# Up-projection of a routed FFN with the weights as stationary operand, fetched tile by tile

## Chip, core and metric

The kernel runs on one core of one Trainium2 chip. The metric is the device time of one execution in microseconds. Below, TensorE is the matrix engine (PE in the rows, PEld for its weight loads, PEldq and PEq for its sequencer), VectorE is DVE, ScalarE is ACT, GpSimd is POOL and SyncE is SP.

## What is computed

A gated cross-attention block over x (2 x 1024 tokens, 256 wide) and 77 text tokens, and behind it a mixture of 8 experts of which each token takes two. All in fp32. Cut to what matters:

```python
# attention: h = tanh(text[t] + feat[s] + b) for every pair, 77 x 1024 x 256 per batch
rho = einsum('bftd,d->bft', tanh(txt_proj + feat_proj + b), w)
att = softmax(rho + mask); txt_h = att @ text
x = x + tanh(g0) * (tanh(txt_h @ Wcw + bcw) * layernorm(x) + tanh(txt_h @ Wcb + bcb))
# experts on n = layernorm(x); H = 1024, D = 256, E = 8, top 2
probs = softmax(n @ router_w.T); vals, idx = top_k(probs, 2)
for eid in range(8):
    w = sum(where(idx == eid, vals, 0))
    out += w * (gelu(n @ w1[eid].T) @ w2[eid].T)
x = x + tanh(g1) * out
```

## The kernel before

The 2048 tokens are taken in four quarters of 512. A quarter of the attention is 40 blocks k = 0 to 39, each with 128 of the 256 features and four text tokens (one in the last pair of blocks): VectorE adds (sum_block, L783), ScalarE takes the tanh (tanh_block, L479 and L481), TensorE reduces over the features (rho_block, L578). hbuf holds four blocks. While quarter q runs, quarter q-1 is settled between the blocks: softmax, gates, the residual, the second layernorm, the router (L598), the places of the rows. The rows are scattered by POOL into row_scratch, sorted by expert (L432), and a table tells the expert (tab_e) and the first row (tab_r) of each tile of 128 rows. Work between blocks stands in tables written out by hand (PE_F, ACT_F, DVE_F, L281 to L286): at block k of its own engine a step of a tile is issued, and each engine goes through its instructions in order.

There are 41 tiles of 128 rows, i = 1 to 41. Tiles 1 to 4 run in the third quarter, 5 to 8 in the fourth, 9 to 14 each in a step written out, interleaved with the settling of the last quarter, and 15 to 41 in a loop of 13 pairs and a last step. All 8 experts' w1 and w2 lie in SBUF (w1_sb, w2_sb, 8 MB each), loaded once near the start, 16 DMAs of 1 MB (L326, L327).

A tile goes through these operations:

- xs_load (L353, SP): SP waits for meta_ok of the tile two before (a buffer of xs is free), loads the row number into a register and fetches 128 rows of 1060 bytes into xs.
- turn_x (L609, TensorE): two transposes to xsT_ps; turned_x (L930, VectorE) copies them to xsT.
- up (L619): in two halves of 512 hidden columns, each two matmuls with xsT as the stationary operand (128x128) and w1 (128x512) moving. The result in h_ps has the rows on partitions and the hidden units along the bank.
- gelu (L496, ScalarE): twice 512 columns, to hg.
- turn_h (L637): eight transposes of hg to hT_ps; turned_h (L945, VectorE) copies them to hgT in two pieces (L948).
- down (L627): eight matmuls with hgT as the stationary operand and w2 (128x256) moving, summed in y_ps.
- y_out (L934, VectorE): y_ps times the router's weight to y_sb, after the previous add has landed. keep_meta (L941) copies the rows' token numbers and weights, after the add two before has landed.
- add (L436, POOL): an indirect DMA adds y_sb to the rows of out.

In the steady part the engines run this order per step i. TensorE (L670): up(i), turn_x(i+1), down(i-1), turn_h(i). VectorE (L1005): turned_x(i+1), keep_meta(i), turned_h(i), y_out(i-1). In the quarters GELU's halves stand behind blocks (6, 7), (13, 14), (21, 22) and (31, 32), the halves of up behind (4, 5), (11, 12), (19, 20) and (29, 30). hT_ps shares its banks with xsT_ps, so turn_x waits for hT_ok.

Behind the last quarter the settling stands in the steps of tiles 9 to 11: scores, gates and x1 in step 9, x2 and a table in step 10, the router's top2 and place in step 11, then the last table (L1024). SP then writes eight tiles of padding rows (L382) into row_scratch, waits for them and for the scattered rows, and loads xs of tile 15.

Of the kernel before, what the change touches and what calls it, by code (L numbers as in the profile page):

```python
# [97 lines left out]
def flamingo_moe(nc, x, ctxT, mask, columns, scalars, Ws, W, router, w1, w2, out):  # L98
    with ExitStack() as ctx:
# [7 lines left out]
        w1_sb = sb("w1_sb", [P, E, DC, H])  # L107
# [65 lines left out]
        hg = sb("hg", [P, H])  # L173
        hgT = sb("hgT", [P, HC, P])
        y_sb = sb("y_sb", [P, D])

        xp = hg[:].rearrange("p (t d) -> p t d", t=TPQ)
        xnT = hgT[:].rearrange("p c d -> p (c d)").rearrange("p (c k) -> p c k", c=DC)
# [66 lines left out]
        xs_in = [sem("xs_in0"), sem("xs_in1")]  # L245
        xsT_ps_ok = sem("xsT_ps_ok")
# [3 lines left out]
        hT_ps_ok = sem("hT_ps_ok")  # L250
        hT_ok = sem("hT_ok")
# [24 lines left out]
        def steps(**at):  # L276
# [36 lines left out]
        def _(sp):  # L313
# [39 lines left out]
            def xs_load(i, par, half):  # L353
# [3 lines left out]
                sp.dma_start(xs[:, par, :], scratch[bass.ds(r, P), :]).then_inc(xs_in[par], 16)  # L357

# [110 lines left out]
        def _(act):  # L469
# [53 lines left out]
            with act.Fori(0, PAIRS) as n:  # L523
                for u in range(2):
                    gelu(tile_pair(n, u)[0], 0)
                    gelu(tile_pair(n, u)[0], 1)
            gelu(TE - 1, 0)
            gelu(TE - 1, 1)

        @block.tensor  # L530
        def _(pe):
# [534 lines left out]
```

## Time and profile before

| | us |
|---|---|
| median of 3 runs | 667.19 |
| lowest, highest | 666.21, 667.31 |
| span of the profiled execution | 666.7 |

| engine | busy us | share | instructions |
|---|---|---|---|
| TensorE, matmuls | 564.8 | 85% | 2850 |
| TensorE, weight loads | 291.3 | 44% | 2851 |
| VectorE | 405.9 | 61% | 1176 |
| ScalarE | 366.9 | 55% | 365 |
| GpSimd | 114.5 | 17% | 98 |

How to read it: a busy share is a mean over stages with different limits. The ends of matmuls are modelled, so a duration of one matmul is longer than its share of a dense stream; distances between starts tell more. Weight loads overlap matmuls. One fp32 matmul is two records, one fp32 transpose is one. Line numbers are those of the kernel. In the timeline a row is: start us, busy us, engine, line, operation, out<-in, shapes, count, and in brackets the idle time before it and what released it; instructions of one kind in a row are merged, and the matmul's duration of a merged row goes from its first start to its last end.

### The profile page before, as it was taken

To read this page: it belongs to the slowest core of one execution; us is meant where nothing else is said; L and a number is where in the kernel's file an instruction comes from. 1 tells how busy PE (TensorE), PEld (TensorE's weight loads), DVE (VectorE), ACT (ScalarE), POOL (GpSimd) and SP (SyncE) were. 2 spreads that over 40 slices of the span, in tenths; PEclk is the share of its full clock that TensorE was granted. 3 is DMA by queue.
4 is the path that set the end of the run, shared out by engine and by line. 5 is a ranking of instruction groups with operands and counts; after the bars stand their busy time and mean duration, and the time that the engine had idled before them with its cause. 6 is when DMAs were issued, how large, how long until landed. Compare 5 with 4: busy or idle time off the path is not lost.

```text
span 666.7 us, 9922 instructions
## 1 busy us (share of the span) xinstructions
PE 564.8 (85%) x2850; PEld 291.3 (44%) x2851; DVE 405.9 (61%) x1176; ACT 366.9 (55%) x365; POOL 114.5 (17%) x98
## 2 busy tenths in 40 slices
PE   3777685766679988889979988699999999999993
PEld 2312121120123432333333565467777666666773
DVE  4899988988868897788887565122222333222321
ACT  0699999999997997998999312011111111111110
POOL 2000000013001160101250115111111111122111
PEclk9798999698999997899999999799999999999998
DMA  3006993002002012102030133312222221221221
GB/s 117 32 1 250 421 403 72 33 17 97 0 1 49 9 67 56 17 0 47 12 102 23 17 65 95 85 19 38 33 32 32 33 39 32 32 32 32 33 28 19
DMA packets 26426, 42.02 MB, mean 63 GB/s; under 512 B 3840, under 2 KB 23296, under 8 KB 24352
## 3 DMA queue, kind: packets, MB, share of 16 engines
q1 hardware_dynamic: 18768, 31.72, 14.2%
q0 software_dynamic: 7632, 9.98, 9.4%
q8 instruction: 13, 0.21, 0.1%
q14 instruction: 13, 0.11, 0.1%
HBM read 27.31 MB, written 14.38 MB: 63 GB/s over the span
## 4 chain that ended last, share of the span: by engine, by line
PE 45%; issue 14%; DVE 9%; ACT 4%; DMA 4%; POOL 3%; SPq 2%; DVEq 1%; ACTq 0%; POOLq 0%
PE y_bank L632 18%; PE h_ps L622 16%; PE rho L578 5%; PE hT_ps L643 4%; DVE hbuf L783 3%; DMA out<-y_sb,meta 2%; ACT hbuf L479 2%; POOL row_scratch L432 2%; ACT hbuf L481 1%; PE hT_ps L616 1%; DMA xs<-row_scratch 1%; DMA row_scratch<-rows,slot 1%; PE misc L598 1%; POOL out L442 1%; SPq L381 1%
## 5 line engine op out<-in xcount | busy, mean ns | idle before, releaser
L479 ACT ACTIVATE hbuf<-hbuf 128x1536 f32<-128x1536 f32 (+2 forms) x160 | 248.0, 1577 | 31.5 <-DVE hbuf L783 31.2
L783 DVE TENSOR_SCALAR hbuf<-featT,txtb 128x512 f32<-128x512 f32 (+1 forms) x519 | 214.7, 481 | 22.0 <-PE rho L578 21.2
L578 PE MATMUL rho<-hbuf,wpad 128*32 128x512 f32 x1232 | 176.5, 648 | 52.7 <-ACT hbuf L481 29.4
L498 ACT ACTIVATE hg<-h_ps 128x512 f32<-128x512 f32 x82 | 48.8, 596 | 228.6 <-PE h_ps L622 225.4
L632 PE MATMUL y_bank<-w_sb,hgT 128*128 x672 | 158.0, 387 | 2.3 <-DVE y_sb L939 1.6
L622 PE MATMUL h_ps<-w_sb,xsT 128*128 x328 | 151.0, 599 | 0.2
L632 PEld LDWEIGHTS y_bank<-w_sb,hgT 128*128 128x128 f32 x672 | 125.8, 193 | 31.0 <-issue 15.4
L442 POOL DMA_INDIRECT out<-y_sb,meta x42 | 67.7, 1612 | 382.4 <-DVE y_sb L939 309.8
L578 PEld LDWEIGHTS rho<-hbuf,wpad 128*32 128x32 f32 x1232 | 29.3, 112 | 162.9 <-ACT hbuf L481 76.9
L622 PEld LDWEIGHTS h_ps<-w_sb,xsT 128*128 128x128 f32 x328 | 58.6, 191 | 70.2 <-issue 70.2
L948 DVE COPY hgT<-hT_ps 128x512 f32<-128x512 f32 x82 | 52.8, 686 | 46.7 <-PE hT_ps L643 46.0
L481 ACT ACTIVATE hbuf<-featT,txtb 128x512 f32 (+1 forms) x97 | 68.6, 707 | 0.0
L932 DVE COPY xsT<-hT_ps 128x256 f32<-128x256 f32 x41 | 17.4, 424 | 78.8 <-PE hT_ps L616 72.8
L643 PE MATMUL hT_ps<-ident,hg 128*128 128x128 f32 x328 | 43.0, 274 | 1.1 <-DVE xsT L932 1.1
L432 POOL DMA_INDIRECT row_scratch<-rows,slot x32 | 35.2, 1099 | 45.4 <-DVE slot L890 36.9
L943 DVE COPY meta<-xs 128x9 f32<-128x9 f32 x41 | 7.2, 175 | 58.3 <-DMA out<-y_sb,meta 58.3
L643 PEld LDWEIGHTS hT_ps<-ident,hg 128*128 128x128 f32 x328 | 37.7, 141 | 11.3 <-issue 6.7
L939 DVE TENSOR_SCALAR y_sb<-y_bank,meta 128x256 f32<-128x256 f32 x42 | 20.3, 483 | 15.4 <-PE y_bank L632 6.1
L616 PE MATMUL hT_ps<-ident,xs 128*128 128x128 f32 x82 | 17.1, 291 | 13.2 <-DMA xs<-row_scratch 12.9
L616 PEld LDWEIGHTS hT_ps<-ident,xs 128*128 128x128 f32 x82 | 11.0, 147 | 36.6 <-issue 24.4
L567 PE MATMUL misc<-hgT,W_sb 128*128 128x512 f32 x32 | 17.6, 685 | 4.3 <-DVE hgT L770 4.3
L420 POOL TENSOR_TENSOR rstd<-var,negh 128x4 f32<-128x4 f32 x4 | 4.6, 1143 | 67.7 <-DVE var L759 67.7
(125 smaller groups left out, 203.2 us busy)
## 6 DMA issues: line engine op xcount, KB each, us to landing
w_sb<-in_w SPq DMA_DIRECT2D x16, 1024.0 KB, 21.9
xs<-row_scratch SPq DMA_DIRECT2D x41, 132.5 KB
row_scratch<-pad SPq DMA_DIRECT2D x17, 132.5 KB, 18.4
hg<-in_x SPq DMA_DIRECT2D x4, 512.0 KB, 3.5
x_res<-in_x SPq DMA_DIRECT2D x4, 512.0 KB, 4.7
out<-x_res SPq DMA_DIRECT2D x4, 512.0 KB
out<-y_sb,meta POOLq DMA_INDIRECT x42
row_scratch<-rows,slot POOLq DMA_INDIRECT x32
```

The costliest lines, as they stand in the source:

```text
L432: g.indirect_dma_start(out=scratch, out_offset=bass.IndirectOffsetOnAxis(ap=slot[:, k, t:t + 1], axis=0), in_=rows[:, t, :], in_offset=Non ...
L442: g.indirect_dma_start(out=out, out_offset=bass.IndirectOffsetOnAxis(ap=meta[:, par, 0:1].bitcast(I32), axis=0), in_=y_sb[:], in_offset=No ...
L479: ins = s.activation(h, h, ACT.Tanh)
L481: ins = s.activation(hbuf[:, k % HB, j, :], featT[:, c, bass.ds(q, 1), :].rearrange("p o t -> p (o t)"), ACT.Tanh, bias=txtb[:, c, bb, CG ...
L498: s.activation(hg[:, 512 * c:512 * (c + 1)], h_ps[:, 512 * c:512 * (c + 1)], ACT.Gelu).then_inc(hg_ok, 1)
L578: ins = t.matmul(rho[32 * j:32 * j + 32, :], wpad[:, c, 31 - r:63 - r], hbuf[:, k % HB, j, :], start=(k == 0), stop=(last and c == DC - 1) ...
L616: ins = t.transpose(xsT_ps[:, c * P:(c + 1) * P], xs[:, par, c * P:(c + 1) * P], ident[:])
L622: ins = t.matmul(h_ps[:, 512 * c2:512 * (c2 + 1)], xsT[:, c, :], w1_sb[:, bass.ds(e, 1), c, 512 * c2:512 * (c2 + 1)], start=(c == 0), stop ...
L632: ins = t.matmul(y_ps, hgT[:, c, :], w2_sb[:, bass.ds(e, 1), c, :], start=(c == 0), stop=(c == HC - 1))
L643: ins = t.transpose(hT_ps[:, c * P:(c + 1) * P], hg[:, c * P:(c + 1) * P], ident[:])
L783: ins = v.tensor_scalar(hbuf[:, k % HB, j:j + 1, :], featT[:, c, bass.ds(q, 1), :], txtb[:, c, bb, CG * r + j:CG * r + j + 1], None, ALU.add)
L948: v.tensor_copy(hgT[:].rearrange("p c k -> p (c k)")[:, 512 * c2:512 * (c2 + 1)], hT_ps[:, 512 * c2:512 * (c2 + 1)]).then_inc(hT_ok, 1)
```

## The change

The activated tile is produced with the hidden units on partitions, the form in which down needs it. up has w1 as the stationary operand and the turned rows xsT as the moving one: per tile 16 matmuls of 128x128 with 128 columns moving, eight chunks k of 128 hidden units. So turn_h, turned_h, hg, hT_ps and their semaphores are gone; hgT gets two buffers. gelu is one instruction over 1024 columns, placed where its first half stood, and waits for y_ok as well, since it now writes hgT. w1 no longer lies in SBUF as a whole: w1_st holds two tiles' worth, and SP fetches the 1 MB of a tile's expert behind the tile's rows, after gelu of the tile two before. up waits for that fetch and no longer loads the expert into a register. xsT_ps has a bank of its own, and turn_x waits for xsT_ok.

```diff
-        w1_sb = sb("w1_sb", [P, E, DC, H])
+        w1_st = sb("w1_st", [P, 2, DC, H])
-        hg = sb("hg", [P, H])
-        hgT = sb("hgT", [P, HC, P])
+        hgT = sb("hgT", [P, 2, HC, P])
-        hT_ps = bank("hT_ps", 2)
+        xsT_bank = bank("xsT_bank")
-        PE_F = steps(up0=(4, 11, 19, 29), up1=(5, 12, 20, 30), down0=(7, 14, 22, 32), down1=(8, 15, 23, 33),
-                     turn_h=(9, 17, 25, 35))
+        PE_F = steps(up0=(4, 11, 19, 29), up1=(5, 12, 20, 30), down0=(7, 14, 22, 32), down1=(8, 15, 23, 33))
-        ACT_F = steps(gelu0=(6, 13, 21, 31), gelu1=(7, 14, 22, 32))
-        DVE_F = steps(x=(10, 17, 30, 35), meta=(9, 16, 27, 36), y=(12, 19, 28, 37), h=(14, 21, 29, 39))
+        ACT_F = steps(gelu=(6, 13, 21, 31))
+        DVE_F = steps(x=(10, 17, 30, 35), meta=(9, 16, 27, 36), y=(12, 19, 28, 37))
@@ SP
-                sp.dma_start(w1_sb[:, e], w1[:, e]).then_inc(w_in, 16)
...
                 sp.dma_start(xs[:, par, :], scratch[bass.ds(r, P), :]).then_inc(xs_in[par], 16)
+                e = sp.value_load(tab_e[0:1, bass.ds(i, 1)], min_val=0, max_val=E - 1)
+                if not (isinstance(i, int) and i <= 2):
+                    sp.wait_ge(hg_ok, i - 1)
+                sp.dma_start(w1_st[:, par], w1[:, bass.ds(e, 1)].rearrange("p o c m -> p (o c) m")).then_inc(w1_in[par], 16)
@@ ScalarE
-            def gelu(i, c):
-                act.wait_ge(h_ps_ok, 2 * (i - 1) + c + 1)
-                s.activation(hg[:, 512 * c:512 * (c + 1)], h_ps[:, 512 * c:512 * (c + 1)],
-                             ACT.Gelu).then_inc(hg_ok, 1)
+            def gelu(i, par):
+                act.wait_ge(h_ps_ok, i)
+                act.wait_ge(y_ok, i)
+                s.activation(hgT[:, par].rearrange("p c k -> p (c k)"), h_ps[:], ACT.Gelu).then_inc(hg_ok, 1)
@@ TensorE
-            def up(i, c2, e):
-                pe.wait_ge(xsT_ok, i)
-                for c in range(DC):
-                    ins = t.matmul(h_ps[:, 512 * c2:512 * (c2 + 1)], xsT[:, c, :],
-                                   w1_sb[:, bass.ds(e, 1), c, 512 * c2:512 * (c2 + 1)],
-                                   start=(c == 0), stop=(c == DC - 1))
-                ins.then_inc(h_ps_ok, 1)
+            def up(i, par, count, half):
                 if half == 0:
+                    pe.wait_ge(w1_in[par], 16 * count)
+                    pe.wait_ge(xsT_ok, i)
+                    pe.wait_ge(hg_ok, i)
+                for k in range(HC // 2 * half, HC // 2 * (half + 1)):
+                    for c in range(DC):
+                        ins = t.matmul(h_ps[:, k * P:(k + 1) * P],
+                                       w1_st[:, par, c, k * P:(k + 1) * P], xsT[:, c, :],
+                                       start=(c == 0), stop=(c == DC - 1))
+                if half == 1:
+                    ins.then_inc(h_ps_ok, 1)
...
-            def turn_h(i, x_before=True):
-                if x_before:
-                    pe.wait_ge(xsT_ok, i + 1)
-                for c2 in range(2):
-                    pe.wait_ge(hg_ok, 2 * (i - 1) + c2 + 1)
-                    for c in range(HC // 2 * c2, HC // 2 * (c2 + 1)):
-                        ins = t.transpose(hT_ps[:, c * P:(c + 1) * P], hg[:, c * P:(c + 1) * P], ident[:])
-                    ins.then_inc(hT_ps_ok, 1)
@@ VectorE
-            def turned_h(i):
-                for c2 in range(2):
-                    dve.wait_ge(hT_ps_ok, 2 * (i - 1) + c2 + 1)
-                    v.tensor_copy(hgT[:].rearrange("p c k -> p (c k)")[:, 512 * c2:512 * (c2 + 1)],
-                                  hT_ps[:, 512 * c2:512 * (c2 + 1)]).then_inc(hT_ok, 1)
```

down waits for hg_ok instead of hT_ok and reads hgT[:, par].

## Rows read from the trace of the kernel before

**Rows 1.** Stage windows (stretch, length, engines' busy us, clock, DMA), and the page's chain.

```profile
245.00:350.00 105.00, 89.83 (x518) 34.55 (x518) 86.24 (x253) 93.87 (x88) 21.40 (x16) 0.94 0.16 40
435.00:500.00 65.00, 65.00 (x277) 45.38 (x277) 18.97 (x40) 9.57 (x16) 12.40 (x8) 0.99 0.20 31
...
PE y_bank L632 18%; PE h_ps L622 16%; PE rho L578 5%; PE hT_ps L643 4%; DVE hbuf L783 3%; DMA out<-y_sb,meta 2%; ACT hbuf L479 2%; POOL row_scratch L432 2%; ACT hbuf L481 1%; PE hT_ps L616 1%; DMA xs<-row_scratch 1%; DMA row_scratch<-rows,slot 1%; PE misc L598 1%; POOL out L442 1%; SPq L381 1%
```

**Rows 2.** Timeline of one steady step, 559 to 569 us.

```profile
559.32 1.55 POOL L442 DMA_INDIRECT out<-y_sb,meta  x1 [6.44 <-DVE y_sb L939]
...
560.59 3.62 PE L632 MATMUL y_bank<-w_sb,hgT 128*128 x16
...
563.00 0.17 DVE L943 COPY meta<-xs 128x9 f32<-128x9 f32 x1 [1.78 <-DMA out<-y_sb,meta]
...
564.05 1.04 PE L643 MATMUL hT_ps<-ident,hg 128*128 128x128 f32 x8
...
564.92 3.60 PE L622 MATMUL h_ps<-w_sb,xsT 128*128 x8
...
566.04 0.48 DVE L939 TENSOR_SCALAR y_sb<-y_bank,meta 128x256 f32<-128x256 f32 x1
...
567.29 1.55 POOL L442 DMA_INDIRECT out<-y_sb,meta  x1 [6.43 <-DVE y_sb L939]
...
568.36 0.38 PE L616 MATMUL hT_ps<-ident,xs 128*128 128x128 f32 x2
```

**Rows 3.** Window from down's start to down's start, L948's copies alone on VectorE.

```profile
440.84:640.43 199.59, 32.24 (x50) 1.00 0.21 34
```

**Rows 4.** Timeline of router and gate projection, and both by line (busy us, mean ns).

```profile
393.76 1.86 PEld L598 LDWEIGHTS misc<-rT,x2T 128*128 128x128 f32 x16 [1.82 <-DVE x2T L850]
...
20.68 1.25 PE L548 MATMUL h_ps<-x2T,x_res 128*128 128x160 f32 x8
...
L598 PEld LDWEIGHTS misc<-rT,x2T 128*128 128x128 f32 x64 | 7.4, 191 | 5.4 <-DVE x2T L850 5.4
...
L548 PE MATMUL h_ps<-x2T,x_res 128*128 128x160 f32 x8 | 1.2, 299 | 0.0
```

**Rows 5.** Timeline of the third quarter: up1 and GELU of tiles 3 and 4.

```profile
233.30 1.98 PE L622 MATMUL h_ps<-w_sb,xsT 128*128 x4
...
234.32 0.60 ACT L498 ACTIVATE hg<-h_ps 128x512 f32<-128x512 f32 x1
...
259.74 0.60 ACT L498 ACTIVATE hg<-h_ps 128x512 f32<-128x512 f32 x1 [1.99 <-PE h_ps L622]
...
260.63 1.98 PE L622 MATMUL h_ps<-w_sb,xsT 128*128 x4
...
262.65 0.60 ACT L498 ACTIVATE hg<-h_ps 128x512 f32<-128x512 f32 x1 [0.51 <-PE h_ps L622]
```

**Rows 6.** Timeline of the third quarter: ScalarE behind two hgT copies.

```profile
216.59 1.49 ACT L479 ACTIVATE hbuf<-hbuf 128x1536 f32<-128x1536 f32 x1 [1.42 <-DVE hbuf L783]
```

**Rows 7.** Timeline of the stretch behind the last quarter, 380 to 437 us.

```profile
380.30 0.48 DVE L939 TENSOR_SCALAR y_sb<-y_bank,meta 128x256 f32<-128x256 f32 x1
...
381.53 1.56 POOL L442 DMA_INDIRECT out<-y_sb,meta  x1 [14.51 <-DVE y_sb L939]
...
386.72 0.17 DVE L943 COPY meta<-xs 128x9 f32<-128x9 f32 x1 [0.87 <-DMA out<-y_sb,meta]
...
429.07 0.69 PE L616 MATMUL hT_ps<-ident,xs 128*128 128x128 f32 x2 [6.16 <-DMA xs<-row_scratch]
...
429.92 6.56 PE L632 MATMUL y_bank<-w_sb,hgT 128*128 x16 [0.16 <-issue]
```

**Rows 8.** Timeline of the end: y_out of tile 40.

```profile
653.58 0.48 DVE L939 TENSOR_SCALAR y_sb<-y_bank,meta 128x256 f32<-128x256 f32 x1
```

**Rows 9.** DMA issues (KB each, us to landing) and the page's GB/s by slice.

```profile
hg<-in_x SPq DMA_DIRECT2D x4, 512.0 KB, 3.5
...
GB/s 117 32 1 250 421 403 72 33 17 97 0 1 49 9 67 56 17 0 47 12 102 23 17 65 95 85 19 38 33 32 32 33 39 32 32 32 32 33 28 19
```

More of the change, by code:

```diff
@@ L506, in quarter @@
                     if tiles and k in ACT_F:
-                        m, step = ACT_F[k]
-                        gelu(tile(q, m)[0], int(step[-1]))
+                        gelu(*tile(q, ACT_F[k][0])[:2])
             quarter(0, 0, False, False)
@@ L524, in _ @@
                 for u in range(2):
[L525 to L528, printed above, removed]
+                    gelu(*tile_pair(n, u)[:2])
+            gelu(*tile_at(TE - 1)[:2])
         @block.tensor
@@ L607, in settle, with turn_x @@
                              stop=True).then_inc(count_ps_ok, 1)
-            def turn_x(i, par, half, late=False):
+            def turn_x(i, par, half):
                 pe.wait_ge(xs_in[par], 16 * half)
-                if late:
-                    pe.wait_ge(hT_ok, 2 * i)
-                elif not (isinstance(i, int) and i == 1):
-                    pe.wait_ge(hT_ok, 2 * (i - 1))
+                if not (isinstance(i, int) and i == 1):
+                    pe.wait_ge(xsT_ok, i - 1)
                 for c in range(DC):
@@ L658, in quarter @@
                     if k in PE_X and (tiles or settling and k == max(PE_X)):
-                        turn_x(*tile(q, PE_X[k] + 1), late=(PE_X[k] == LATE))
+                        turn_x(*tile(q, PE_X[k] + 1))
                     if tiles and k in PE_F:
                         m, step = PE_F[k]
-                        i = tile(q, m)[0]
+                        i, par, count = tile(q, m)
                         if step in ("up0", "up1"):
-                            up(i, int(step[-1]), expert(i))
-                        elif step in ("down0", "down1"):
-                            down(i - 1, int(step[-1]), expert(i - 1))
+                            up(i, par, count, int(step[-1]))
                         else:
-                            turn_h(i, x_before=(m != LATE))
+                            down(i - 1, 1 - par, int(step[-1]), expert(i - 1))
             def step(this, following, mid=lambda: None, late=lambda: None):
-                i = this[0]
-                e = expert(i)
-                up(i, 0, e)
-                up(i, 1, e)
+                i, par, count = this
+                up(i, par, count, 0)
+                up(i, par, count, 1)
                 mid()
@@ L678, in step @@
                 e = expert(i - 1)
-                down(i - 1, 0, e)
-                down(i - 1, 1, e)
+                down(i - 1, 1 - par, 0, e)
+                down(i - 1, 1 - par, 1, e)
                 late()
-                turn_h(i, bool(following))
             pe.wait_ge(setup_sb, DC)
```

34 lines of the change are left out of this document (14 added, 20 removed).

## The prediction

> **What bounds the kernel now.** I read the stage windows first. Up to 370 us the tanh blocks set the pace: from 245 to 350 us ScalarE is busy 93.87 of 105 us, TensorE 89.83, VectorE 86.24, so two other engines stand close behind. From 435 us on TensorE is busy in all of the stage while ScalarE and VectorE are mostly idle, at a granted clock of 0.99 (2.4 GHz) [rows 1]. The chain that ended last says the same: the down-projection (L632) 18% and the up-projection (L622) 16% lead it [rows 1]. So I cost the parts one by one: the 26 steady expert steps behind 437 us, the end, the seam from 370 to 437 us, and the two tiled quarters before it.
>
> **The steady step, before.** The starts of TensorE's groups in one step of the timeline give down(i-1) 560.59 to 564.05 = 3.46 us, turn_h 564.05 to 564.92 = 0.87, up 564.92 to 568.36 = 3.44, and turn_x the rest [rows 2]. The window from one down-projection's start to another holds 50 hgT copies, two a tile, so 25 tiles in 199.59 us: 7.98 us a step [rows 3]. turn_x is 7.98 - 3.46 - 0.87 - 3.44 = 0.21 us. None of the four waits for data.
>
> **The steady step, after.** turn_h goes (-0.87 us), turn_x stays, down keeps its 16 records at 3.46 us (its moving side and weights have the same shapes). An fp32 matmul is two records. up had 4 matmuls, 8 records in 3.44 us, 0.43 us each for 512 columns; it gets 16 matmuls, 32 records of 128 columns. The streaming is the same: 0.43 / 4 = 0.107 us a record, 3.44 us. New is a weight load for every one. The nearest row for a load by itself is the router's, 128x128 fp32 with only 8 columns moving: 16 loads in 1.86 us, one load lasting 0.191, so (1.86 - 0.19) / 15 = 0.111 us apart [rows 4]. The nearest for load beside matmul is the gate projection, 8 records of 160 columns in 1.25 us, one lasting 0.299: (1.25 - 0.30) / 7 = 0.136 us apart, where 160 columns stream in 0.107 x 160 / 128 = 0.134 and a load needs 0.111 [rows 4]. The load is hidden there to 0.002 us. So I take the larger of 0.107 and 0.111: 32 x 0.111 = 3.55 us. Bounds: 0.107 (3.42 us) below; 0.136 above, since 128 columns can hardly take longer than 160 (4.35 us). The step becomes 3.46 + 0.21 + 3.55 = 7.22 us, 0.76 less; between 7.09 and 8.02 by the bounds.
> Twenty-six periods lie between up(15) and up(41): -19.8 us.
>
> What must stay hidden in a step of 7.2 us. GELU in one piece is at most 2 x 0.60 us and can start only when all of up is done; it has the whole down-projection, 3.46 us, before up(i+1) wants h_ps and down(i) wants hgT. Its new wait for y_ok is no later than the one that down(i-1) had already. The two hgT copies (1.29 us a tile) go from VectorE; in this stage they cost only the place of y_out behind them: y_sb starts at 566.04, 2 us after down ended [rows 2]. The loop of the adding store is y_sb 0.48, to POOL's start 0.77, POOL's start to landing 3.7 (559.32 to 563.00): some 5.0 us [rows 2]. It fits in 7.2 with 2.2 to spare, where it had 3.0.
> The w1 fetch is 1 MB a tile on SP's queue. SP waits for meta_ok, loads a register, issues xs, loads another, waits for hg_ok of the tile two before (done by then) and issues w1. Queued behind that wait on SP are the next xs load and, in the quarters, the loads and stores of x; all are wanted later than the gelu waited for. Its length: the weights' loads of 1 MB ran at 421 GB/s in their fullest slice, 2.5 us for 1 MB, and a 512 KB load landed 3.5 us after issue, so about 4.7 us [rows 9]. It is issued about two steps ahead of its use, less the wait for meta: over 6 us are left. I cost it at nothing. If that cover is gone, up waits for w1 and the excess stands on every step.
>
> **The end.** Now: copies, then y_out(40) at 653.58, its add lands, y_out(41), last add [rows 8]. After, y_out(40) starts right behind down(40), which ended some 1.9 us before 653.58 (turn_h and both copies lie between); the rest follows add by add. -1.9 us.
>
> **The seam.** Here VectorE, in order, carries settle steps, hgT copies, y_out and waits for adds. y_out(8) at 380.30 stood behind two copies (-1.6 us) and its add, landed at 386.72, held back x2, the table and y_out(9); further copies stood before y_out(9) and before place [rows 7]. Walking the same chain without copies and turn_h, with up at 3.55, I get y_out(9) 2.7 us, the counts 2.8 us and the end of the table 5 us earlier. Then SP: xs(14), the eight pads, and xs(15), on whose landing turn_x waited until 429.07 [rows 7]. One more register load and issue (w1 of tile 14) stand in front of the pads: +1.1 us, at a register load and an issue of about 0.5 us each, an estimate. So turn_x(15) comes about 4.2 us earlier; down(13) behind it ran at half rate, 6.56 us [rows 7], and will again, since TensorE idles at least as long before. turn_h(14) after it goes, -0.87. Taken: -5 us. Bounds: 0, if w1 traffic slows the adds on that chain by all of it, and -7.
> In that chain the wait for `added` is what ends last, so the slower add (386.72 - 381.5 = 5.2 us after POOL's start, where it is 3.7 in the steady stage) is already in.
>
> **The two tiled quarters.** Gains: 8 hgT copies a quarter go from VectorE, 5.1 us, and 4 x 0.87 us from TensorE, but neither is the leader; what shows is ScalarE's idle time behind them, such as 1.42 us at 216.59 [rows 6]. I count 1.3 us a quarter. GELU in one piece saves one fixed part, about 0.15 us a tile: 0.6.
> Loss: gelu0 stood after block 6 (13, 21, 31), when only up0 was done; the whole GELU now stands there and needs up1, on TensorE behind block 5 (12, 20, 30). In the third tile up1 runs 233.30 to 235.3 and gelu0 ran at 234.32: 1 us of wait. In the fourth, up1 runs 260.63 to 262.6 and gelu0 ran at 259.74, a tanh block between it and gelu1 at 262.65: that block now comes after, about 2.5 us late [rows 5]. The first two tiles I put at 0.3 us each. Sum 4.1, of which the idle time that follows anyway takes about 0.7. Net per quarter 4.1 - 0.7 - 1.9 = +1.5; for two +3 us. Bounds: -3 (all waits absorbed) and +8 (none, no gain).
> The 8 MB less at the start (w1_sb) frees nothing: TensorE asks for the weights only at the third quarter, behind 180 us, while the slices at 421 and 403 GB/s, the fifth and sixth of 40, end at 100 us [rows 9].
>
> **Sum.** Against the profiled execution's 666.7 us: -19.8 - 1.9 - 5 + 3 = -23.7, so 643.0. The span is within 0.5 us of the median of the runs, 667.19; I leave it there.
>
> **Rivals.** A, slower: the load is not hidden at equal length. Where load and stream take 0.111 and 0.107, any record above (7.98 - 3.46 - 0.21) / 32 = 0.135 us makes the step longer than now. With half of the load bare, 0.107 + 0.055 = 0.162: up 5.2 us, step 8.9, +23 us on 26 steps, and some 1.7 us more on the tiles before, partly hidden: about 690. Against it: the 160-column row, 0.136 with everything in it. Chance 5%.
> The Trainium skill, "TensorE: Matmul & The Clock Gate", section "Back-to-back issue gap", has a rule for this rival: the pace of load-and-matmul pairs is set by both, 81 ns at 128 columns where the isolated gap is 56. By its ratio a record would be 0.107 x 81 / 56 = 0.155 us, the step 8.6 and the time about 680, an estimate from that page. Its figures are not for fp32, and the gate projection's row disagrees.
> B, adds become the bound: w1's 2.5 us of transfer falls on the add's own, since w1 is issued about when the previous add has landed. If each add is longer by all of it, the loop is 5.0 + 2.5 = 7.5 us, the step follows it, -0.5 x 26 = -12 and the seam gives only 3: 666.7 - 12 - 1 - 3 + 3 = about 654. For it: the slower 5.2 us add beside other traffic [rows 7]. Against: the two overlap in part only, and an add that comes late delays the next issue of w1 as well. Chance 14%. The Trainium skill, "Trainium Kernel Development and Optimization", section "Key Constraints", says that DMAs from SP's and POOL's queues run on the same 16 engines and interleave, which speaks for B; by full sharing it is the 654 above.
> C, records between 0.120 and 0.136: step 7.5 to 8.0, time 650 to 663. Chance 8%.
> D, the waits in the quarters and the seam cost more (+8, 0): 653. Chance 8%; the other way, 636 and less: 7%.
>
> **How the numbers follow.** The forecast case (638 to 649) has 56%; A 5%, B 14%, C 8%, D 8%, better 7%, and 2% for a w1 fetch that comes late on every step and makes it slower. The range reaches to B and most of D and C: 635 to 657, which leaves out A and the far ends. A measurement of this kernel tells 0.2% (1.3 us) from no change. Faster by more 0.91, within 0.02, slower by more 0.07.
>
> **What would show it.** In a steady step of the changed kernel: 32 records of up in about 3.5 us and starts of down 7.2 us apart; loads 0.11 us apart; no wait of up on w1; gelu within down; y_sb right behind down. y_sb or the down-projection waiting for the add's landing is B. In the quarters, ScalarE idle before GELU released by h_ps, 1 us in the third tile and 2 to 2.5 in the fourth. The wait for xs(15) should end near 425 us plus what the quarters cost. A step over 7.5 us, or a seam that gains nothing, makes the prediction wrong.

## The result, and the profile after

The median went from 667.19 to 656.74 us (5 runs, 655.15 to 665.18); the ratio to the kernel before is 0.985 with the interval 0.982 to 0.988. So the kernel is faster by 10 us where 24 were forecast. The profiled execution of the changed kernel, with a span of 663.4 us, was the slowest of the five, so every comparison of stages below reads `again`, the very same kernel measured a second time (span 653.3 us, median 655.97).

The page of after first: its engines, the traffic by slice, the groups and the transfers with KB each and the time from issue to landing.

```profile
span 663.4 us, 10960 instructions
...
PE 549.6 (83%) x3506; PEld 355.8 (54%) x3507; DVE 356.0 (54%) x1093; ACT 360.4 (54%) x324; POOL 116.4 (18%) x98
...
GB/s 118 32 1 276 344 26 0 33 17 149 75 1 103 20 67 182 80 0 111 8 73 175 79 112 160 211 161 159 159 161 168 173 186 180 162 159 160 166 151 24
...
L498 ACT ACTIVATE hgT<-h_ps 128x1024 f32<-128x1024 f32 x41 | 42.0, 1025 | 238.8 <-PE h_ps L620 228.4
...
L620 PE MATMUL h_ps<-xsT,w_st 128*128 128x128 f32 x1312 | 164.0, 285 | 0.5 <-DMA w_st<-in_w 0.5
...
w_st<-in_w SPq DMA_DIRECT2D x41, 1024.0 KB, 4.9
...
out<-y_sb,meta POOLq DMA_INDIRECT x42, 5.5
```

The transposes, their records and the 82 hgT copies are gone, GELU is one instruction a tile. But in the 27th to 38th slices 159 to 186 GB/s are moved, where it was 19 to 39 [rows 9], and the store that adds to `out` lands 5.5 us after its issue. Up itself waited for w1 only 0.5 us in all. The step is read from the timeline of `again` (columns: start, length, engine, line, operation; in brackets the idle time before it and what ended it):

```profile
562.26 3.76 PEld L620 LDWEIGHTS h_ps<-xsT,w_st 128*128 128x128 f32 x32
562.48 3.73 PE L620 MATMUL h_ps<-xsT,w_st 128*128 128x128 f32 x32
562.70 0.17 DVE L929 COPY meta<-xs 128x9 f32<-128x9 f32 x1 [3.54 <-DMA out<-y_sb,meta]
563.64 0.48 DVE L925 TENSOR_SCALAR y_sb<-y_bank,meta 128x256 f32<-128x256 f32 x1 [0.76 <-DVE meta L929]
563.70 0.34 SPq L352 DMA_DIRECT2D xs<-row_scratch  x1
564.88 1.55 POOL L441 DMA_INDIRECT out<-y_sb,meta  x1 [6.27 <-DVE y_sb L925]
564.88 0.33 SPq L356 DMA_DIRECT2D w_st<-in_w  x1
...
566.05 0.38 PE L609 MATMUL xsT_bank<-ident,xs 128*128 128x128 f32 x2
566.25 1.02 ACT L498 ACTIVATE hgT<-h_ps 128x1024 f32<-128x1024 f32 x1 [6.71 <-PE h_ps L620]
...
566.72 3.71 PE L631 MATMUL y_bank<-w_sb,hgT 128*128 x16 [0.29 <-issue]
...
570.27 2.17 PE L620 MATMUL h_ps<-xsT,w_st 128*128 128x128 f32 x18
570.75 0.17 DVE L929 COPY meta<-xs 128x9 f32<-128x9 f32 x1 [3.85 <-DMA out<-y_sb,meta]
```

Up takes 566.05 - 562.48 = 3.57 us, 0.112 a record, as forecast. Between turn_x and down stand 0.67 us where [rows 2] have 0.21. And the add that POOL starts at 564.88 lands only at 570.75, 5.87 us later, where [rows 2] have 3.7; w1's fetch is issued in the same hundredth of a microsecond as POOL starts. keep_meta waits for that landing on VectorE, and y_sb stands behind it.

By stage, from the starts of the same instructions in each trace (third and fourth quarter from rhoT to rhoT; seam from the last rhoT to turn_x(16); tail from turn_x(16) to turn_x(41); end from there):

| us | start | quarters | seam | tail (a step) | end | span |
|---|---|---|---|---|---|---|
| before | 180.3 | 97.2 + 92.2 | 71.0 | 199.6 (7.98) | 26.5 | 666.7 |
| again | 181.2 | 94.1 + 94.3 | 66.2 | 192.6 (7.70) | 25.0 | 653.3 |
| difference | +0.9 | -1.0 | -4.8 | -7.0 | -1.5 | -13.4 |
| forecast | 0 | +3 | -4.9 | -19.0 | -2.8 | -23.7 |

The forecast row is the prediction's sum, cut at the same places. Its 26 periods run from up(15) to up(41); 25 of them are the tail here, 25 x 0.76 = 19.0, and the 26th lies in two pieces: up(15) (+0.1) in the seam, turn_h(40) (-0.87) in the end. Of the 10.3 us between forecast and trace, the tail misses 12.0, the end 1.3 and the start 0.9; the quarters came out 4.0 better.

### The profile page after: what moved, and what is told of

Its sections match the earlier page's. It is cut to its first block and busy times, and to the rows that moved or that the text cites. A ratio compares the mean times of both kernels' runs of the same rounds, so it can differ in the third digit from the quotient of the medians.

```text
span 663.4 us, 10960 instructions
## 1 busy us (share of the span) xinstructions
PE 549.6 (83%) x3506; PEld 355.8 (54%) x3507; DVE 356.0 (54%) x1093; ACT 360.4 (54%) x324; POOL 116.4 (18%) x98
## 5 line engine op out<-in xcount | busy, mean ns | idle before, releaser
L498 ACT ACTIVATE hgT<-h_ps 128x1024 f32<-128x1024 f32 x41 | 42.0, 1025 | 238.8 <-PE h_ps L620 228.4
L620 PEld LDWEIGHTS h_ps<-xsT,w_st 128*128 128x128 f32 x1312 | 160.1, 200 | 19.8 <-issue 17.4
L631 PE MATMUL y_bank<-w_sb,hgT 128*128 x672 | 163.6, 396 | 7.6 <-issue 5.6
L620 PE MATMUL h_ps<-xsT,w_st 128*128 128x128 f32 x1312 | 164.0, 285 | 0.5 <-DMA w_st<-in_w 0.5
L918 DVE COPY xsT<-xsT_bank 128x256 f32<-128x256 f32 x41 | 17.4, 424 | 74.0 <-PE xsT_bank L609 73.6
L609 PE MATMUL xsT_bank<-ident,xs 128*128 128x128 f32 x82 | 16.4, 282 | 5.7 <-DMA xs<-row_scratch 5.7
L609 PEld LDWEIGHTS xsT_bank<-ident,xs 128*128 128x128 f32 x82 | 10.1, 144 | 11.8 <-DMA xs<-row_scratch 5.9
L419 POOL TENSOR_TENSOR rstd<-var,negh 128x4 f32<-128x4 f32 x4 | 4.6, 1141 | 66.2 <-DVE var L745 66.2
L423 POOL TENSOR_TENSOR rstd<-var,negh 128x4 f32<-128x4 f32 x4 | 5.5, 1378 | 51.4 <-DVE var L824 51.4
L562 PEld LDWEIGHTS misc<-hgT,W_sb 128*128 128x128 f32 x32 | 6.1, 208 | 14.9 <-issue 8.9
L554 PE MATMUL misc<-ident,rows 128*128 128x128 f32 x32 | 7.5, 411 | 4.5 <-DVE rows L750 4.5
## 6 DMA issues: line engine op xcount, KB each, us to landing
row_scratch<-pad SPq DMA_DIRECT2D x17, 132.5 KB, 10.3
```

The source lines that it names most:

```text
L498: s.activation(hgT[:, par].rearrange("p c k -> p (c k)"), h_ps[:], ACT.Gelu).then_inc(hg_ok, 1)
L562: ins = t.matmul(misc[e][:], W_sb[:, c, e * P:(e + 1) * P], xnT[:, c, :], start=(c == 0), stop=(c == DC - 1))
L609: ins = t.transpose(xsT_ps[:, c * P:(c + 1) * P], xs[:, par, c * P:(c + 1) * P], ident[:])
L620: ins = t.matmul(h_ps[:, k * P:(k + 1) * P], w1_st[:, par, c, k * P:(k + 1) * P], xsT[:, c, :], start=(c == 0), stop=(c == DC - 1))
L631: ins = t.matmul(y_ps, hgT[:, par, c, :], w2_sb[:, bass.ds(e, 1), c, :], start=(c == 0), stop=(c == HC - 1))
```

## The experiments

**The same kernel again**, for a second trace. No edit.

> The changed kernel once more, for a profile at an undisturbed clock. Both theories expect 655 to 657 us. The profile so far shows a steady step of 7.71 us, where 7.22 was forecast, and GELU waiting 10.7 us for h_ps in the third quarter. Theory Q (the quarters lose through the place of the GELU) expects rhoT copies 97 to 100 us apart over the third quarter and 95 to 98 over the fourth, 97.2 and 92.2 before. If the quarters' loss was only the lower clock of that execution, they come back to 97 and 92.

Measured 655.97 us, ratio 0.986 (0.982 to 0.989), the table and fence above. The gain comes back, and the step is 7.7 us also here.

**Without w1's traffic.** The fetch stays where it is with its register load, wait and issue, but moves 16 bytes a partition; two experts' w1 are loaded once near the start. The up-projection so takes the wrong experts' w1 for most tiles.

```diff
-  sp.dma_start(w1_st[:, par], w1[:, bass.ds(e, 1)]...)
+  sp.dma_start(w1_st[:, par, 0, 0:4], w1[:, bass.ds(e, 1), 0, 0:4]...)
```

> w1 of experts 0 and 1 is loaded once, and each tile's fetch is cut from 8 KB to 16 bytes a partition, so its issue, its waits and its place on SP stay and its traffic goes (the output is not the reference's: each tile uses the wrong expert's w1). Theory C (a cycle over two steps: the add lands late beside w1, so keep_meta, so the xs load, so TensorE's sequencer gets to turn_x and to the register load for down too late): the add lands 3.7 to 3.9 us after POOL's start instead of 5.4, xs lands 1.5 us earlier, turn_x to down falls from 0.65 to 0.22 us, the step from 7.71 to 7.24, and the time by 26 x 0.47 = 12 us to about 644. Theory S (TensorE's sequencer alone: 32 short load-and-matmul pairs leave it no lead, so the register load for down is bare whatever the DMAs do): the step stays at 7.7 and the time at 655.

Measured 641.04 us (638.8 to 643.9), ratio 0.963 (0.958 to 0.968); step 7.27, turn_x to down 0.22. From its timeline:

```profile
562.03 0.48 DVE L928 TENSOR_SCALAR y_sb<-y_bank,meta 128x256 f32<-128x256 f32 x1 [1.99 <-PE y_bank L634]
562.04 0.34 SPq L358 DMA_DIRECT2D w_st<-in_w  x1
563.28 1.55 POOL L444 DMA_INDIRECT out<-y_sb,meta  x1 [5.70 <-DVE y_sb L928]
...
567.14 0.17 DVE L932 COPY meta<-xs 128x9 f32<-128x9 f32 x1 [1.72 <-DMA out<-y_sb,meta]
```

The add lands 3.86 us after POOL's start, and y_sb waits for down again. So it is the megabyte, not the extra instructions on SP, that costs the 0.43 us a step. It isn't the place of xs either: xs is issued 1.00 us behind keep_meta here as in `again` (means of the steps between 460 and 610 us). How the megabyte costs it, the run doesn't say.

**The fetch alone, in the kernel before.** Everything as before, but w1 fetched a tile at a time behind xs and used as the moving side.

```diff
   sp.dma_start(xs[:, par, :], scratch[bass.ds(r, P), :])...
+  e = sp.value_load(tab_e[...]); sp.wait_ge(hg_ok, 2 * (i - 2) + 1)
+  sp.dma_start(w1_st[:, par], w1[:, bass.ds(e, 1)]...)
...
-  ... w1_sb[:, bass.ds(e, 1), c, 512 * c2:512 * (c2 + 1)]
+  ... w1_st[:, par, c, 512 * c2:512 * (c2 + 1)]
```

> The kernel before with one part of the change alone: w1 fetched tile by tile into two buffers (SP issues it behind xs, after GELU of the tile two before), up in its old form with w1 moving. Theory P: the fetch lengthens the add here too if w1's transfer falls on it, but the step of 7.98 us leaves room (two steps 15.97 against a cycle of about 15.4 or less), so the step stays at 7.98 to 8.05 and the time at 665 to 669. If the fetch has a cost of its own (its issue on SP, the memory's bandwidth, TensorE's reads beside its writes), the step grows by about the 0.45 us that it cost in the changed kernel, and the time to 677.

Measured 667.79 us (666.64 to 668.3), ratio 1.002 (1.000 to 1.004); step 7.98, the add 3.78 us. The same megabyte per tile costs nothing here. What differs is its place:

```profile
563.68 0.34 SPq L362 DMA_DIRECT2D w_st<-in_w  x1
...
565.66 1.55 POOL L447 DMA_INDIRECT out<-y_sb,meta  x1 [6.43 <-DVE y_sb L945]
```

POOL starts 2 us behind w1's issue; in `again` they coincide.

**One part each: a later GELU, and the sequencer's wait.** TensorE's gap before down looked like a cause: its sequencer passes the wait for xs late and the register load for down's expert lies bare behind it. `hoist` loads that register ahead; `late_gelu` moves GELU one block later in the quarters.

```diff
-  ACT_F = steps(gelu=(6, 13, 21, 31))
+  ACT_F = steps(gelu=(7, 14, 22, 32))      # late_gelu
-  if following: turn_x(*following)
   e = expert(i - 1)
+  if following: turn_x(*following)         # hoist
```

> ACT_F places the GELU of a tile one block later, where its second half stood (7, 14, 22, 32). Theory Q: the waits of GELU for h_ps in the quarters (10.7 us in the third) fall to below 2 us, the quarters give back 2 to 3 us each, time 650 to 652. If instead TensorE or VectorE sets the quarters' pace, the wait only moves and the time stays within 1.5 us of 656.

> TensorE's register load for the expert of down stands ahead of turn_x instead of behind it. Cycle theory: TensorE's sequencer gets through the wait for xs only just before turn_x, and the register load behind it is bare, 0.65 us from turn_x to down against 0.22. With the load ahead of the wait, turn_x to down is 0.22 us; the cycle over two steps is 0.43 us shorter, so the step goes from 7.70 to about 7.49, with the rest of the wait now in front of turn_x; time 655.5 - 5 = 650. If the gap is a wait for something else (y_ok, hg_ok), it stays at 0.65 and the time at 656.

late_gelu 655.58 us (0.985, 0.980 to 0.991), hoist 656.44 us (0.985, 0.983 to 0.987): neither moves the time. In hoist the gap is gone, and up waits instead:

```profile
564.13 3.81 PE L620 MATMUL h_ps<-xsT,w_st 128*128 128x128 f32 x32 [0.29 <-DMA w_st<-in_w]
564.59 0.17 DVE L929 COPY meta<-xs 128x9 f32<-128x9 f32 x1 [3.77 <-DMA out<-y_sb,meta]
...
565.53 0.48 DVE L925 TENSOR_SCALAR y_sb<-y_bank,meta 128x256 f32<-128x256 f32 x1 [0.76 <-DVE meta L929]
565.59 0.34 SPq L352 DMA_DIRECT2D xs<-row_scratch  x1
566.77 1.55 POOL L441 DMA_INDIRECT out<-y_sb,meta  x1 [6.27 <-DVE y_sb L925]
566.77 0.33 SPq L356 DMA_DIRECT2D w_st<-in_w  x1
```

The step stays at 7.75: TensorE's waits are symptoms of something that turns with a period of its own.

**w1 issued first.** SP issues w1 (wait hg_ok) ahead of the wait for meta_ok and xs.

```diff
+  e = sp.value_load(...); sp.wait_ge(hg_ok, i - 1); sp.dma_start(w1_st[:, par], ...)
   r = sp.value_load(...); sp.wait_ge(meta_ok, i - 1)
   sp.dma_start(xs[:, par, :], ...)
-  e = sp.value_load(...); sp.wait_ge(hg_ok, i - 1); sp.dma_start(w1_st[:, par], ...)
```

> Only SP's order is turned round: w1 of a tile is issued first (after its wait for GELU), then the tile's xs (after its wait for keep_meta). So far: with the fetch's traffic away the steady step is 7.27 us, with xs loaded early it is 7.25, and in both the add lands 3.8 us after POOL's start (5.55 in the changed kernel, where w1 is issued at the moment of POOL's start). Theory P (phase: what costs is that w1's transfer falls on the add's; issued right behind GELU it is over before the add begins): add to landing 3.8, step 7.25, time 643 to 645, although xs is loaded no earlier relative to its keep_meta. Theory X (what costs is that xs is asked for late, behind keep_meta; early_xs gained by that): xs comes as late as now or later, step 7.6 to 7.8, time 653 to 656.

Measured 658.79 us, ratio 0.988 (0.985 to 0.991): no gain as a whole, where theory P had 643 to 645 us. But the add is 3.80 us, and 21 of the tail's 25 steps are 7.24 to 7.53 us; three of 8.1 to 8.2 bring the mean to 7.43 (7.70 in `again`). The quarters and the seam took back what the tail gave (fourth quarter 98.9, seam 71.1; 94.3 and 66.2 in `again`). In the new order xs has to wait for GELU of two tiles before too, which would explain that; it was not tried apart. From the timeline:

```profile
562.38 1.55 POOL L441 DMA_INDIRECT out<-y_sb,meta  x1 [5.91 <-DVE y_sb L925]
...
565.08 0.33 SPq L352 DMA_DIRECT2D w_st<-in_w  x1
566.27 0.17 DVE L929 COPY meta<-xs 128x9 f32<-128x9 f32 x1 [1.74 <-DMA out<-y_sb,meta]
```

A fetch issued 2.7 us behind POOL's start no longer slows that add, and its own landing is early enough for the next.

**xs freed early.** keep_meta's source is copied behind turned_x, so SP needn't wait for the add.

```diff
-  sp.wait_ge(meta_ok, i - 1)
+  sp.wait_ge(xs_free, i - 2)
   v.tensor_copy(xsT..., xsT_ps).then_inc(xsT_ok, 1)
+  v.tensor_copy(metaq[:, par, :], xs[:, par, D:ROW]).then_inc(xs_free, 1)
-  v.tensor_copy(meta[:, par, :], xs[:, par, D:ROW])
+  v.tensor_copy(meta[:, par, :], metaq[:, par, :])
```

> VectorE copies the rows' tokens and weights out of xs right behind turned_x into a pair of small buffers, so xs is free, and its next load issued, without waiting for an add; keep_meta copies from there. Theory C: the two-step cycle is cut; what is left is the add's own loop, y_sb 0.48 + 0.76 to POOL + 5.4 to landing + 0.17 + 0.79 of register load before the next y_sb = 7.6 us, so the step falls only from 7.71 to about 7.6, unless w1's earlier issue changes the overlap; turn_x to down falls to 0.22. Time about 653. Theory S: turn_x to down stays at 0.65 and the time at 656.

> The kernel of early_xs once more: its four executions came at 642.6, 647.0, 672.1 and 675.1 us, in two groups. If the two groups belong to the kernel, they come back here, some executions near 645 and some near 673; theory P then has a second state of the phase, in which w1 falls on the add in each step. If they belonged to that chip's minute, all come near 645.

Executions were 646.99, 672.12, 642.64, 675.07 us, and the second time 649.5, 646.47, 672.27, 647.2: two groups of the same program, 25 us apart, so no single number stands for it. Both profiles are of the short group: step 7.245, add 3.77 us.

**VectorE's register load.** Behind keep_meta's wait a register load lies bare (0.76 us in `again`). `y_hoist` puts it ahead of y_out's waits, but still behind keep_meta's; `y_hoist_early` joins that with hoist and the early xs, `y_hoist_early_late` with late_gelu besides.

```diff
+  e = dve.value_load(tab_e[...])
   dve.wait_ge(y_ps_ok, i + 1); dve.wait_ge(added, 16 * (i + 1)); dve.wait_ge(meta_ok, i + 1)
-  e = dve.value_load(tab_e[...])
```

> In y_out VectorE loads the expert's number into a register ahead of its waits instead of behind them; nothing else. Theory A (the adding store's own loop sets the step: y_sb's start to POOL's start 1.24, POOL's start to keep_meta 5.55, keep_meta to the next y_sb 0.94, together 7.73, measured steps 7.70 to 7.75 in four kernels): the 0.94 falls to about 0.2, the loop to 7.0, and the step to what comes next, 7.25 to 7.35; time 645 to 648. Theory W (the landing of w1, issued behind xs behind keep_meta, sets it; the kernel with TensorE's register load moved showed up waiting for w1): y_sb's place hardly matters, the step falls by a third of 0.7 at most, to 7.5, time 651 or more.

> early_xs with both register loads (TensorE's for down, VectorE's for y_out) ahead of their waits. In steps where w1 doesn't fall on the add the step is TensorE's own 7.25 already, so nothing is gained there. Theory A: the second group of early_xs (672 to 675 in 3 of 8 executions) is a state in which the add's loop sets the step; with the loop 0.7 us a step shorter, that group comes down by about 18 us or goes, and all executions lie between 642 and 656. If the second group is a matter of something else, it comes back at 670 or more.

> The kernel of y_hoist_early with the GELU of the quarters one block later as well. The quarters varied from 92 to 101 us each between executions, with a granted clock of 0.93 to 1.00 in the shorter and 0.80 to 0.83 around the third tile's up in the longer ones; there up at half rate held up a GELU that ScalarE's next tanh waited behind. With a block of tanh before the GELU the long quarters should come down by 2 to 3 us; in the short ones nothing changes (the kernel with this edit alone gave 0). Time 640 to 646, and at least not above y_hoist_early.

y_hoist 655.79 us (0.984, 0.982 to 0.986): the load stayed bare behind keep_meta (0.95 us from keep_meta to y_sb), so the run doesn't test theory A. The other two split again: 673.8, 670.36, 641.07, 639.99 and 669.43, 674.19, 673.18, 637.76 us. This time the profile of y_hoist_early caught the long group:

```profile
562.29 0.17 DVE L935 COPY meta<-metaq 128x9 f32<-128x9 f32 x1 [6.50 <-DMA out<-y_sb,meta]
...
563.26 0.48 DVE L930 TENSOR_SCALAR y_sb<-y_bank,meta 128x256 f32<-128x256 f32 x1 [0.79 <-DVE meta L935]
...
563.84 1.02 ACT L500 ACTIVATE hgT<-h_ps 128x1024 f32<-128x1024 f32 x1 [7.34 <-DVE y_sb L930]
...
564.50 1.55 POOL L443 DMA_INDIRECT out<-y_sb,meta  x1 [6.81 <-DVE y_sb L930]
565.03 0.34 SPq L358 DMA_DIRECT2D w_st<-in_w  x1
...
570.62 0.17 DVE L935 COPY meta<-metaq 128x9 f32<-128x9 f32 x1 [6.47 <-DMA out<-y_sb,meta]
```

A ring: the landing lets keep_meta go, y_sb follows 0.97 us later, y_sb releases GELU (its new wait for y_ok) after 0.58, GELU's hg_ok lets SP issue w1 after 1.19, and the next add lands 5.59 us after w1's issue: 8.33 us, against a mean step of 8.43. Here GELU and down both wait for y_sb, so it holds the fetch and the matmuls. The profile of y_hoist_early_late, of its 669.43 us execution, shows the same: a mean step of 8.44, w1 issued 0.5 us behind POOL, the add 6.2 us long. The sum alone proves no ring, for the add's own loop, from keep_meta over y_sb and POOL to the landing, closes on the same length (0.95 + 1.28 + 6.23 us). Taking a link out tells more.

**GELU without the wait for y_ok**, on the early-xs kernel; the down-projection of two tiles before, which read the same hgT, stands ahead of up on TensorE anyway.

```diff
-  act.wait_ge(y_ok, i)
```

> early_xs without GELU's wait for y_ok (hgT's buffer is free without it: down of two tiles before stands ahead of this tile's up on TensorE). In the long executions of early_xs's kind the step was 8.43 us = 1.24 + 6.24 + 0.95, the add's loop, with GELU released by y_sb and w1 issued 0.5 us behind POOL's start. Theory L (that is a lock: landing, y_sb, GELU, w1's issue, w1's transfer on the next add): without the wait w1's issue follows up and not y_sb, the lock has no hold, and all executions lie between 641 and 650. Without truth in L, some executions still come at 670 or more.

Six executions, 642.18 to 650.49 us, median 647.62, ratio 0.964 (0.961 to 0.967), none in the long group, where 8 of the 16 of the three kernels with that wait and the early xs were. Nor was one in the long group among the nine of `best` and `best_old_gelu` below, which lack the wait too. That supports the ring: with one link taken out, it wasn't seen in 15 executions. They can't exclude it.

**Which ring holds the changed kernel?** Two were left. (A) landing, keep_meta, register load, y_sb, POOL, landing. (K) landing, keep_meta, SP's register load and xs, SP's second register load and w1, and the next add landing some 5.6 us after w1's issue, if POOL started about then. `e_ahead` shortens A alone, by loading VectorE's register at the head of the step; `sp_ahead` shortens K alone, by loading SP's two registers ahead of its wait for meta_ok.

```diff
+  e = expert(i - 1)                # e_ahead: at the head of the step, ahead of keep_meta
...
+  r = sp.value_load(...); e = sp.value_load(...)    # sp_ahead
   sp.wait_ge(meta_ok, i - 1)
-  r = sp.value_load(...)
   sp.dma_start(xs[:, par, :], ...)
-  e = sp.value_load(...)
   sp.wait_ge(hg_ok, i - 1); sp.dma_start(w1_st[:, par], ...)
```

> The changed kernel with y_out's register load ahead of keep_meta's wait too (y_hoist had left it behind that one, and 0.78 us from keep_meta to y_sb stayed). Theory A: the add's loop, 1.24 + 5.55 + 0.94 = 7.73 us, loses about 0.7; POOL's start comes before w1's issue instead of with it, so the add does not get longer: the step falls to 7.25 to 7.35 and the time to 644 to 648. Theory W (w1's or xs's landing sets the step): only the part of their chain that goes through y_sb gets shorter, 0.7 in three steps: step 7.5, time 650 to 652.

> SP loads both register values (row and expert) ahead of its wait for keep_meta, nothing else. Theory K (e_ahead, where y_sb came 0.7 us earlier and the add 0.7 us longer at the same step of 7.7, speaks for it): the cycle runs through SP and not through y_sb: w1's issue to the add's landing 5.6 us, which lands only with w1, landing to xs's issue 1.0, to w1's issue 1.18, together 7.8. Without the two register loads the 2.18 become some 1.0 to 1.4 us, the cycle 6.6 to 7.0, and the step TensorE's own 7.25; time 644 to 647. Theory A (the add's loop through y_sb): w1's issue comes forward onto the add or ahead of it, but y_sb's loop has the same members, step 7.6 to 7.75, time 654 to 657.

e_ahead: 655.65 us, ratio 0.978 (0.976 to 0.981) to a kernel before that took 670.33 beside it. y_sb did come 0.7 us earlier, and the step stayed, 7.69: the add grew by just that. From its timeline:

```profile
560.03 1.55 POOL L441 DMA_INDIRECT out<-y_sb,meta  x1 [6.18 <-DVE y_sb L928]
560.73 0.33 SPq L356 DMA_DIRECT2D w_st<-in_w  x1
...
566.40 0.17 DVE L932 COPY meta<-xs 128x9 f32<-128x9 f32 x1 [3.53 <-DMA out<-y_sb,meta]
566.62 0.48 DVE L928 TENSOR_SCALAR y_sb<-y_bank,meta 128x256 f32<-128x256 f32 x1
567.40 0.34 SPq L352 DMA_DIRECT2D xs<-row_scratch  x1
```

The landing is 6.37 us behind POOL and 5.67 behind w1. Ring A is out. sp_ahead: 644.48 us (641.88 to 649.63), ratio 0.966 (0.961 to 0.972):

```profile
560.39 0.17 DVE L929 COPY meta<-xs 128x9 f32<-128x9 f32 x1 [1.80 <-DMA out<-y_sb,meta]
560.74 0.33 SPq L353 DMA_DIRECT2D xs<-row_scratch  x1
...
561.26 0.33 SPq L356 DMA_DIRECT2D w_st<-in_w  x1
561.42 3.73 PE L620 MATMUL h_ps<-xsT,w_st 128*128 128x128 f32 x32
562.44 0.48 DVE L925 TENSOR_SCALAR y_sb<-y_bank,meta 128x256 f32<-128x256 f32 x1 [1.88 <-PE y_bank L631]
563.69 1.55 POOL L441 DMA_INDIRECT out<-y_sb,meta  x1 [5.70 <-DVE y_sb L925]
...
564.99 0.38 PE L609 MATMUL xsT_bank<-ident,xs 128*128 128x128 f32 x2
...
565.21 3.62 PE L631 MATMUL y_bank<-w_sb,hgT 128*128 x16
...
567.45 0.17 DVE L929 COPY meta<-xs 128x9 f32<-128x9 f32 x1 [1.62 <-DMA out<-y_sb,meta]
...
568.66 3.73 PE L620 MATMUL h_ps<-xsT,w_st 128*128 128x128 f32 x32
```

w1 follows keep_meta by 0.87 us, not 2.18, and POOL starts 2.4 us behind w1. The add takes 3.76 us, y_sb waits for down, and the step is 3.57 + 0.22 + 3.45 = 7.24 us, with all the traffic still there. Moving two register loads, and nothing else, brings back what was missing. xs comes 0.65 us sooner behind keep_meta as well, but it stood at 1.00 in nofetch, with a step of 7.27. That is K.

The first steps of the tail of `again` show the ring taking hold:

| POOL's start, us | w1's issue, us before (-) or behind (+) it | add lands after, us | to POOL's next start, us |
|---|---|---|---|
| 434.34 | -1.54 | 3.87 | 7.34 |
| 441.68 | -1.29 | 4.16 | 7.24 |
| 448.92 | -0.93 | 4.56 | 7.26 |
| 456.18 | -0.53 | 5.07 | 7.30 |
| 463.48 | -0.07 | 5.47 | 7.64 |
| 471.12 | +0.01 | 5.69 | 7.87 |

At first TensorE sets the pace, 7.25 us, and w1 is out ahead of the add. But the next w1 comes 2.16 us after the landing, and the landing 5.4 to 5.7 us after w1, more than 7.25 together: each w1 slips towards POOL's start, and each add lands later. It stops where y_sb waits for keep_meta too. From there w1 and POOL hang on the same landing, 2.16 and 0.94 + 1.27 = 2.21 us behind it. That is why they coincide.

**Together.** `best` is e_ahead, hoist, late_gelu, the early xs and GELU without the y_ok wait; `best_old_gelu` is the same without late_gelu.

> early_nowait with VectorE's register load ahead of keep_meta, TensorE's ahead of turn_x, and the GELU of the quarters one block later. If A and L hold, the add's loop is about 6.3 us with w1's transfer out of its way and 7.0 to 7.7 with it, the step is TensorE's own 7.25 in all executions, and the time 638 to 646 with no second group.

> The kernel best with the GELU of the quarters back at blocks 6, 13, 21 and 31. best took 634.4 us, with quarters of 92.1 and 90.7 us at a granted clock of 0.93 to 1.00; early_nowait took 647.6 with 100.1 and 98.1, the same step of 7.245. If the place of the GELU makes the difference, this kernel's quarters are 95 us or longer and its time 641 to 648; if it doesn't (alone in the changed kernel it gave nothing), the time is within 2 us of 634.

best: 634.4 us (633.6 to 636.65), ratio 0.948 (0.946 to 0.950), the fastest of all kernels here; it leaves no work out. best_old_gelu: 638.83 us, 0.954 (0.950 to 0.958). Both have a step of 7.245; the two profiles differ in the quarters (92.1 + 90.7 and 96.5 + 99.2). Since the intervals touch and late_gelu alone gave nothing, it isn't settled that late_gelu is worth those 4 us.

## Why the prediction was right or wrong

The measured 656.74 us lies at the slow edge of the range, 635 to 657, and outside the forecast case, 638 to 649. Term by term:

- **Up at 0.111 us a record**: right (3.57 us for 3.55), so rivals A and C are out. The Trainium skill, "TensorE: Matmul & The Clock Gate", section "Back-to-back issue gap", would by its ratio have made a record 0.155 us, an estimate; the trace shows 0.112 for fp32, and the trace decides.
- **GELU in one piece**: 1.025 us and within down, right.
- **"The w1 fetch ... I cost it at nothing", with "over 6 us left"**: this step failed, and with it the 7.22 us step. The fetch is issued 570.27 - 564.88 = 5.39 us before up needs it, 0.5 us more than the 4.9 that it takes to land: hidden as a wait of up, as forecast, but with 0.5 us left and not 6. And the sum looked only at up. SP's two register loads and issues behind keep_meta take 2.18 us (562.70 to 564.88), and that put the fetch on top of the add, whose landing is what keep_meta waits for. The ring is 2.16 + 5.64 = 7.80 us (means of the steps between 460 and 610 us in `again`), longer than TensorE's 7.24. That these two add up to the step proves nothing, they do in every kernel; that they hold it is shown by their not giving way (5.6 with POOL starting with w1 or 0.7 before it) and by sp_ahead, where 2.16 became 0.87 and the step TensorE's own. Over the tail, whose first four steps are still 7.24 to 7.30, the mean is 7.70, 0.46 a step above 7.24, 12 us in 25. In before_fetch, where keep_meta to w1 is 2.27 us, the same ring would be about 2.3 + 5.6 = 7.9 us, an estimate from these two traces: just under TensorE's step of 7.98, so nothing showed it.
- **"The loop of the adding store ... 5.0 us, fits with 2.2 to spare"**: its add of 3.7 us became 5.6. This is rival B in kind, 14%, 654 us forecast and 656 measured. B priced the add at +2.5 by full sharing; it was +1.8. B's ring, through y_sb, lacked the 0.94 us from keep_meta to y_sb, and with it is as long in the trace (0.94 + 1.27 to POOL + 5.59 = 7.80); but e_ahead took 0.7 us out of it and the step stayed. B's objection, that a late add also delays the next w1, is no relief but the ring itself. That its 654 lies so near is partly luck: its step gained 12 us where the tail gained 7.0, and the seam (-3, measured -4.8) and the quarters (+3, measured -1.0) made up for it. The Trainium skill, "Trainium Kernel Development and Optimization", section "Key Constraints", has SP's and POOL's transfers interleave on the same 16 engines; the trace fits it, an add of 5.6 us for 3.8, though no run looks at a single engine.
- **The seam** -5: measured -4.8, but by two errors that cancel. turn_x(15) came at 426.25 for 429.07, 2.8 us earlier and not 4.2. And down(13) behind it, which the prediction had at the same half rate again, took 427.20 to 432.17 = 4.97 us for 429.92 to 436.32 = 6.40: the granted clock over it was 0.71, in before 0.55, after TensorE had idled 5.52 and 6.16 us. That is luck.
- **The end**: -1.5 where -2.8 belonged (-1.9 and turn_h(40)). y_sb of tile 40 was to start right behind down(40). It starts 640.37 - 635.96 = 4.41 us after down(40)'s start, for 5.39 in before: 1.0 less and not 1.9. In y_hoist and e_ahead, with VectorE's register load ahead of the waits, it is 3.77: 0.64 us was that load, bare.
- **The quarters** +3: -1.0. ScalarE's groups between 180 and 372 us show how far each term was off; of before first, then of `again`:

```profile
L479 ACT ACTIVATE hbuf<-hbuf 128x1536 f32<-128x1536 f32 (+2 forms) x80 | 122.4, 1549 | 12.4 <-DVE hbuf L783 12.4
...
L498 ACT ACTIVATE hg<-h_ps 128x512 f32<-128x512 f32 x16 | 9.4, 590 | 3.9 <-PE h_ps L622 3.9
```

```profile
L478 ACT ACTIVATE hbuf<-hbuf 128x1536 f32<-128x1536 f32 (+2 forms) x80 | 122.1, 1547 | 5.7 <-DVE hbuf L769 5.5
...
L498 ACT ACTIVATE hgT<-h_ps 128x1024 f32<-128x1024 f32 x8 | 8.2, 1024 | 10.9 <-PE h_ps L620 10.9
```

  GELU's waits for h_ps grew by 7.0 (forecast 2 x 4.1), GELU itself fell by 1.2 (2 x 0.6); the idle time of the tanh blocks fell by 6.7, where 2 x (0.7 + 1.3) = 4.0 was forecast. GELU waited 1.14 us in the third quarter's third tile and 2.96 in its fourth, where 1 and 2.5 were forecast. The mechanism was right, that last term too small. Single traces of this stage scatter, though: in that of `after` GELU's waits were 20.6 us, the quarters 198.2, at a granted clock of 0.81 from 230 to 255 us (0.93 in `again`).

Still open: why one execution of an early-xs kernel falls into its 8.4 us ring and another doesn't, and late_gelu's share in `best`.

## What to carry to other kernels

When a prefetch is added, two questions beside its own deadline: which small transfer is in flight when it is issued, and does that transfer's landing decide when the next prefetch is issued. If so, add up the ring (landing, waits, register loads, issues, landing) and hold it against the step; a step made shorter elsewhere can fall below a ring that was harmless. A register load behind a wait is part of the ring if the ring goes through that engine: SP's two, moved ahead of the wait, gave 11 us, while TensorE's (hoist) and VectorE's (e_ahead), moved alone, gave nothing. And a waiting engine that stops waiting without the time moving is a symptom.

## What the hardware showed that was not expected

- How long the 128-row add takes with 1 MB beside it depends on the moment to a fraction of a microsecond. Means over the steps between 460 and 610 us of each timeline:

| kernel | w1's issue after POOL's start | POOL's start to landing | w1's issue to landing |
|---|---|---|---|
| sp_ahead | -2.5 | 3.82 | 6.37 |
| before_fetch | -1.9 | 3.78 | 5.69 |
| again | 0.0 | 5.59 | 5.64 |
| e_ahead | +0.7 | 6.24 | 5.63 |
| y_hoist_early | +0.5 | 6.24 | 5.74 |
| w1_first | +2.7 | 3.80 | |

  As far as these rows go, the add lands 3.8 us after POOL's start or some 5.6 us after the fetch's issue, whichever is later, unless the fetch comes 2.7 us behind POOL. Why the transfers order themselves so wasn't measured.
- A register load and issue on SP take 1.18 us from one issue to the next (563.70 to 564.88 in `again`), 0.52 with the load done before (sp_ahead); the prediction's estimate was about 1.1.
- One program can have two times 25 us apart (early_xs, measured twice: 642.6 to 649.5 and 672.1 to 675.1 us). The traces of two long executions, of y_hoist_early and y_hoist_early_late, show a step of 8.4 us that the short ones lack; the long executions of early_xs left no trace.
